# Convolving attention as 32-row strips: one 128-wide product per head replaced by 16 products of 32x32

## The reference

```python
attn = jnp.einsum('bhqd,bhkd->bhqk', q, k) * scale
...
kernels = jax.nn.softmax(kp.reshape(B, H, K1 * K2), axis=-1).reshape(B * H, 1, 3, 3)
attn0 = jnp.where(mask, 0.0, attn).reshape(1, B * H, T, T)
attn = lax.conv_general_dilated(attn0, kernels, window_strides=(1, 1), padding=((1, 1), (1, 1)),
                                feature_group_count=B * H, ...)
attn = jnp.where(mask, -jnp.inf, attn.reshape(B, H, T, T))
p = jax.nn.softmax(attn, axis=-1)
out = jnp.einsum('bhqk,bhkd->bhqd', p, v)
```

## Time and profile before

| what | value |
|---|---|
| median of 3 runs | 2318.37 us |
| the profiled execution, span of its instructions | 2345.7 us |
| TensorE busy, share of the span | 84% |
| stage "heads1", first to last instruction | 584.2 to 1138.6 us |

### The profile page before, as it was taken

The page is one execution under the profiler, slowest core; times in us unless marked ns, Lnnn a source line. Parts: engine busy times, 40 slices in busy tenths (PEclk is TensorE's granted clock), DMA queues, the critical chain, the costliest instruction groups (busy, mean ns, idle before and its releaser), DMA issues. The chain is left out here.

```text
span 2345.7 us, 41465 instructions
## 1 busy us (share of the span) xinstructions
PE 1968.9 (84%) x13179; PEld 1588.6 (68%) x13201; DVE 1255.6 (54%) x4235; ACT 921.3 (39%) x2196; POOL 776.1 (33%) x1055
## 2 busy tenths in 40 slices
PE   6859999987899999999849988994793797797594
PEld 5747766665798889989749975653582675454593
DVE  2542225633788888888420027975345445784423
ACT  3633321523233333333423345763342344575320
POOL 1012211110444444445211134410555646541132
PEclk9959999988899999999969999995896999899697
DMA  3213221000501110110069964426576475643294
GB/s 138 109 61 124 62 83 43 16 19 23 64 20 33 33 29 20 33 28 2 8 233 342 346 202 113 112 54 252 151 168 244 140 164 121 103 96 121 72 345 141
DMA packets 173404, 261.88 MB, mean 112 GB/s; under 512 B 23184, under 2 KB 138896, under 8 KB 169104
## 3 DMA queue, kind: packets, MB, share of 16 engines
q1 hardware_dynamic: 152272, 209.30, 28.0%
q0 software_dynamic: 16704, 45.64, 8.5%
q10 hardware_dynamic: 4224, 4.33, 0.9%
HBM read 181.19 MB, written 37.75 MB: 93 GB/s over the span
## 5 line engine op out<-in xcount | busy, mean ns | idle before, releaser
L2222 PE MATMUL heads_ps_c<-heads_band,heads_sT 128*128 128x129 f32 x3072 | 370.7, 277 | 13.3 <-DVE heads_band L2447 12.2
L2222 PEld LDWEIGHTS heads_ps_c<-heads_band,heads_sT 128*128 128x128 f32 x3072 | 356.9, 193 | 23.2 <-issue 21.3
L508 POOL DMA_INDIRECT weights_xg<-xn_rows,token_of x197 | 190.3, 966 | 444.8 <-DVE token_of L698 169.9
L2385 POOL TENSOR_SCALAR heads_band<-heads_shifts,heads_taps 128x130 f32<-128x130 f32 x384 | 253.1, 673 | 243.4 <-PE heads_ps_c L2222 239.8
L2315 ACT ACTIVATE heads_probs<-heads_mixes,heads_least 128x256 f32<-128x256 f32 x256 | 116.1, 500 | 344.9 <-DVE heads_least L2460 344.9
L2447 DVE SCALAR_TENSOR_TENSOR heads_band<-heads_shifts,heads_taps,heads_band 128x130 f32<-128x130 f32 x768 | 226.8, 351 | 19.0 <-POOL heads_band L2385 14.4
L1893 ACT ACTIVATE heads_probsT<-heads_ps_e 128x512 f32<-128x512 f32 x256 | 148.0, 597 | 70.0 <-PE heads_ps_e L1736 62.9
L1047 PE MATMUL experts_ps_g<-weights_w,experts_xT 128*128 x504 | 137.1, 396 | 9.1 <-ACT experts_xT L1097 6.9
L1070 PE MATMUL experts_ps_y<-weights_w,experts_hT 128*128 (+1 forms) x486 | 135.2, 387 | 4.3 <-ACT experts_hT L1111 1.7
L1712 PE MATMUL heads_ps_m<-heads_stackK,heads_stackQ 96*128 96x256 bf16 x512 | 101.3, 283 | 31.0 <-DMA heads_stackQ<-heads_q_pieces 12.4
L1104 ACT ACTIVATE experts_silu<-experts_ps_g 128x128 f32<-128x128 f32 (+1 forms) x165 | 53.3, 323 | 162.7 <-PE experts_ps_u L1052 77.8
(11 more groups left out here) (425 smaller groups left out, 4178.9 us busy)
## 6 DMA issues: line engine op xcount, KB each, us to landing
experts_w<-in_experts_dram SPq DMA_DIRECT2D x23, 2180.0 KB
weights_w<-in_experts_dram SPq DMA_DIRECT2D x32, 768.0 KB
weights_w<-in_experts_dram SPq DMA_DIRECT2D x14, 1536.0 KB
y_rows<-experts_y SPq DMA_DIRECT2D x125, 128.0 KB
heads_stackK<-heads_k_pieces SPq DMA_DIRECT2D x192, 64.0 KB, 2.7
heads_stackQ<-heads_q_pieces SPq DMA_DIRECT2D x192, 64.0 KB, 2.5
weights_w<-in_experts_dram SPq DMA_DIRECT2D x8, 1088.0 KB
xn_rows<-xn SPq DMA_DIRECT2D x4, 2048.0 KB, 7.5
```

The costliest lines, as they stand in the source:

```text
L508: pool.indirect_dma_start(self.xg[:, u, :], None, xn_dram, bass.IndirectOffsetOnAxis(ap=tb.token_of[:, j:j + 1], axis=0)).then_inc(self.x_ ...
L2222: last = pe.matmul(out[:, qc * SEQ + k0:qc * SEQ + k1], sT[:, h % 2, kc, qc * P + dq:qc * P + dq + P], band[:, h % 2, dq, w0:w0 + k1 - k0] ...
L2385: last = pool.tensor_scalar(band[:, h % 2, dq, :], shifts[:, 0, :], taps[:, r % 2, h, dq * TAPS:dq * TAPS + 1], None, ALU.mult)
```

## The change

The stage is written anew with strips. A sequence's 256 query rows are eight strips of 32 rows of which the inner 30 are kept, and a ninth that yields the last 16. A strip of one head lies on 32 partitions, four heads fill 128, and the band is a 32x32 matrix per tap column, so that a convolution is products of 32 rows by 32 columns: four heads on the array's four row groups, four strips on its four column groups. A step is four heads of a sequence (32 steps), or the ninth strips of all 16 heads of a sequence (8 steps). Scores come out with queries on partitions. ScalarE takes projections out of PSUM, GpSimd splits all rounds but the first two and builds the bands of a whole sequence at once. `ps_w` has four banks, `ps_s` two, `ps_o` (projections, values, mixes, turning back) and `ps_t` (transposes) one each. The context copies go; the loops are unrolled; the mask input grows from 1024 to 3072 bytes a partition; the inputs of the earlier shared-expert stage get a stage scope of their own.

```diff
-            def convolve(i, H):
...
-                        for dq in range(TAPS):
-                            last = pe.matmul(out[:, qc * SEQ + k0:qc * SEQ + k1],
-                                             sT[:, h % 2, kc, qc * P + dq:qc * P + dq + P],
-                                             band[:, h % 2, dq, w0:w0 + k1 - k0], ...)
+    STEPS = [(b, a) for b in range(B) for a in (None, 0, 1, 2, 3)]
+    pairs_of = lambda s: 2 if STEPS[s][1] is None else 4
...
+            def score(n, m):
...
+                if k >= 2:
+                    pe.wait_ge(masked, k - 1)
+                for half in range(2):
...
+                    for g in range(GH):
...
+                        last = pe.matmul(ps_s[LANE * g:LANE * (g + 1), k % 2, half * SEQ:(half + 1) * SEQ],
+                                         stackQ[:, u % SLOTS, first:first + LANE], stackK[:, u % SLOTS, j, :], ...)
+            def convolve(n):
+                pe.wait_ge(masked, pairs_before(n + 1))
...
+                for dk in range(TAPS):
+                    for g in range(GH):
+                        if dk == 0:
...
+                                pe.wait_ge(drained, 4 * (n - 1) + g + 1)
+                        rows = slice(LANE * g, LANE * (g + 1))
+                        for c in range(4):
...
+                                out = ps_w[LANE * c:LANE * (c + 1), g, :].rearrange("p (w n) -> p w n", w=2)
+                                band = bands[rows, b % 2, a, dk, :]
+                                src = sN[rows, group_of(n) % 2, c:c + 5:4, dk:dk + SEQ]
+                            last = pe.matmul(out, band, src, start=(dk == 0), stop=(dk == TAPS - 1), ...)
```

More of the change, by code:

```diff
@@ new lines, in conv_heads_stage @@
+        mask_add = s.sb("mask_add", [P, 3, SEQ])
+        near, taps = s.sb("near", [P, TAPS, LANE]), s.sb("taps", [P, B * GROUPS, TAPS * TAPS])
+        bands, product = s.sb("bands", [P, 2, GROUPS, TAPS, LANE]), s.sb("product", [P, 2, GROUPS, TAPS, LANE])
+        sN, sN9 = s.sb("sN", [P, 2, WINDOWS, SEQ + 2]), s.sb("sN9", [P, GROUPS, SEQ + 2])
+        mixes, probs, probsT = (s.sb(n, [P, GH, 2 * SEQ]) for n in ("mixes", "probs", "probsT"))
+        p9 = s.sb("p9", [P, GH, QC, GROUPS, NINTH])
@@ L2165, in _ @@
+            for u in range(ROUNDS):
+                stack(u, 0)
+                if u >= 2:
+                    stack(u, 1)
         @block.tensor
         def _(pe):
[L2167 to L2174, removed]
-                pe.wait_ge(v_placed, u + 1)
[L2176 to L2183, removed]
@@ L2240, in mix, with project @@
[L2240 to L2249 removed]
+            def project(u, n, out):
+                b, p = u // 2, u % 2
+                for c in range(DC):
+                    last = pe.matmul(out, (wq, wk)[n][:, c, p * P:(p + 1) * P], xnT[:, c, b * SEQ:(b + 1) * SEQ],
+                                     start=(c == 0), stop=(c == DC - 1))
+                last.then_inc(projected, 1)
@@ new lines, in _, with build_bands @@
+            steps.done(last)
+            def build_bands(b):
+                if b >= 2:
+                    pool.wait_ge(convolved, 4 * 5 * (b - 1))
+                shape = [P, GROUPS, TAPS, LANE]
+                tap = lambda dq: taps[:, GROUPS * b:GROUPS * (b + 1), dq * TAPS:(dq + 1) * TAPS].unsqueeze(3)\
+                    .to_broadcast(shape)
+                eye = lambda dq: near[:, dq, :].unsqueeze(1).unsqueeze(1).to_broadcast(shape)
+                band = bands[:, b % 2, :, :, :]
+                for dq, to in ((0, band), (1, product[:, 0, :, :, :]), (2, product[:, 1, :, :, :])):
+                    last = pool.tensor_tensor(to, tap(dq), eye(dq), ALU.mult)
+                steps.done(last)
+                for n in range(2):
+                    last = pool.tensor_tensor(band, band, product[:, n, :, :, :], ALU.add)
+                    if n == 0:
+                        steps.done(last)
+                last.then_inc(band_ready, 1)
@@ new lines, in drain @@
+            def drain(n, g):
+                v.wait_ge(convolved, 4 * n + g + 1)
+                if n > 0:
+                    v.wait_ge(exped, 4 * (n - 1) + g + 1)
+                for half in range(1 if STEPS[n][1] is None else 2):
+                    columns = slice(half * SEQ, (half + 1) * SEQ)
+                    last = v.tensor_tensor_reduce(out=mixes[:, g, columns], in0=ps_w[:, g, columns],
+                                                  in1=mask_add[:, 2 if STEPS[n][1] is None else half, :], scale=1.0,
+                                                  scalar=-NEG_BIG, op0=ALU.add, op1=ALU.min,
+                                                  accum_out=least[:, g, half:half + 1])
+                last.then_inc(drained, 1)
@@ L2490, in _ @@
-            for r in range(3):
-                for part in range(5):
-                    split(0, r, part)
-            loop(0, SLOTS)
-            first, per_loop = steps.n, ALL + SLOTS
-            with v.Fori(1, LOOPS - 1) as i:
-                steps.n = first + per_loop * (i - 1)
-                loop(i, SLOTS)
-            steps.n = first + per_loop * (LOOPS - 2)
-            loop(LOOPS - 1, 1)
-            row_max(LOOPS - 1, ALL - 1)
-            finish(LOOPS - 1, SLOTS - 1)
+                last.then_inc(finished, 1)
@@ new lines, in _ @@
+            v.wait_ge(edges_ready, 1)
+            for m in range(2):
+                drop_masked(0, m)
+            for n in range(len(STEPS) + 1):
+                before = STEPS[n - 1] if n else None
+                if n + 1 < len(STEPS):
+                    drop_masked(n + 1, 0)
+                    drop_masked(n + 1, 1)
+                if n < len(STEPS):
+                    drain(n, 0)
+                    drain(n, 1)
+                if n + 1 < len(STEPS) and pairs_of(n + 1) > 2:
+                    drop_masked(n + 1, 2)
+                    drop_masked(n + 1, 3)
+                if n < len(STEPS):
+                    drain(n, 2)
+                    drain(n, 3)
+                if before and before[1] in (1, 3):
+                    finish(group_of(n - 1) // 2)
```

690 lines of the change are left out of this document (366 added, 324 removed).

## The result

The changed kernel takes 2170.58 us (median of 4 runs, 2164.30 to 2171.71) against 2318.89 for the one before: a ratio of 0.9359, 95% interval 0.9344 to 0.9374. The forecast was 2145 with a range of 2095 to 2260. The saving is 148 us where 175 was forecast. The profiled execution before lay 27 us over the median of its runs, and that excess lies behind the changed stage (1207.1 us from the stage's end on, against 1180.4 in the trace after), so the stages of the two traces can be set against each other.

What follows compares the result with a forecast made beforehand. TensorE was taken to bound the stage: 23.5 start + 339 steps + 6 end = 368.5 for 554.4 us, 186 less; minus 10 for gaps and 1 for a boundary, 175 saved from 2318.4, said as 2145, range 2095 to 2260.

Steps and rivals of the forecast that it cites:

- What bounds the stage: In the convolving body of heads1 TensorE decides, 513.7 of 527.2 us; waits of VectorE, GpSimd or ScalarE cost nothing.
- The convolution: On TensorE, four heads' regular convolution takes 2.58 us, six rounds of 0.43 with all 16 products at once; a ninth 1.29.
- The chain of a step: TensorE and ScalarE hand over through single-bank tiles: a step 9.2 us with a = 2, 9.9 with a = 1 and 3.
- My 10 us for unexplained gaps: Taken off the stage's forecast saving of 186 us, for gaps that no wait explains.
- Rival 1: Row groups of a convolution don't overlap: 10.3 us each, 279 us more, 2424 us in all; chance 10%.
- Rival 2: Row groups overlap in part, eight products at once: convolution 5.16 us, 93 us more, 2238 in all; chance 15%.
- Rival 3: The clock falls because TensorE waits in every step: at 1.2 GHz half the time, 118 us more, 2263; chance 8%.

Runs made afterwards that it cites:

- two other orders of the places: Two edits of the changed kernel: column groups looped outside row groups, 2169.24 us; the second tap column's products in reverse order, 2167.15 us.
- copying twice: Changed kernel with ScalarE making each copy of turned probabilities in a regular step a second time, into a spare tile first: 2213.64 us.
- moving the scores: Changed kernel with the two scores that stand last in a step put ahead of the second head's transposes: 2153.76 us.

## Why the prediction was right, and its sizes

**What bounds the stage** was right. The time came out of TensorE's products. VectorE's 242 us and GpSimd's 159 us of work that went didn't count: 81 us put back on VectorE cost 2, while up to eight products at once in place of sixteen cost 110. No run put work back on GpSimd; for it there is only that no wait of TensorE in the view above ends with it.

**The convolution** was mis-sized. I took 6 rounds of 0.43 and a result 2.85 us after the start; it took 3.40, and a ninth one 2.13 for some 1.58. That is 0.55 in 40 steps, 22 of the 27 us by which the saving fell short. The working went from one row with four at once, and that row gave no hint: its 32 records are four products one after the other on each of four places, each with weights of its own, which load while the records before still run (timeline of the kernel before):

```profile
506.84 0.13 PEld L2682 LDWEIGHTS shared_ps_a<-shared_z,shared_w_cols 128*32 128x32 f32 x4 [0.30 <-issue]
...
507.27 0.13 PEld L2682 LDWEIGHTS shared_ps_a<-shared_z,shared_w_cols 128*32 128x32 f32 x4 [0.30 <-issue]
```

There the rounds stay 0.43 us apart through every new product, and so they do for a single row group of 32 rows (2.78 us a head). With sixteen at once each new tap column costs 0.19, and what comes once is 0.44, not 0.27. In the step above one load of the second tap column runs at 731.16 and the next only from 731.59 on, 0.88 us after the convolution's start. Why the others don't run earlier, as they do in the row of before, stays open: two other orders of the places made no difference.

96 records one after the other would be, by estimate from the rounds, 96 x 0.43 = 41.3 us and 0.16 by which the last outlasts its distance to the next (0.59 and 0.43). The measured 3.40 us is 12.2 times as fast. The Trainium skill, "TensorE: Matmul & The Clock Gate", Part 3, "Measured speedup vs the span model", has 10.6 for sixteen; by it the forecast was 2192 as against my 2145, and the measured 2171 lies between the two. The measurement decides: for these f32 products, in six rounds, it is 12.2.

**The chain of a step** was right in every link, as the timeline above shows, and copying twice and moving the scores agree with it from both sides. Behind the convolution it was 0.33 us too short in the step with a = 2: half of that lies in three changes of the array's shape (mix to transposes 1.00 us for 0.96, transposes to scores 0.59 for 0.54, scores to convolution 0.55 for 0.47), most of the rest in transposes whose result came after 0.66 us and not 0.60. A sequence is 47.15 us (the ninth convolutions start at 656.89 and 704.03) for 43.1, and the last two 44.87 for 40.1: 372.6 for 339. My 10 us for unexplained gaps cover a third of that, by luck: they were meant for something else and are as large as what the steps lack beside the convolutions (32 x 0.33). With the first convolution 25.3 us into the stage for 23.5 this makes the 25 us by which the stage is longer than forecast (404.1 for 379.5).

**Rival 1** (row groups in series) didn't come: the records stand 16 at a time. Issued in series the row groups still overlapped by two, for 2310; kept apart, they came with the lower clock, for 2808. Its price holds by the estimate from single heads: 11.4 us a convolution at the upper level for my 10.3, 289 us more than sixteen at once for my 279.

**Rival 2** (partial overlap) named 5.16 us for eight at once. Up to eight at once took 6.50; the changed kernel's 3.40 is far nearer to the 2.85 forecast for sixteen.

**Rival 3** (the clock falls) didn't come in the changed kernel: 1.0 from 615.0 to 983.6 us, with 44 us of gaps. The runs with fewer row groups at once did have the lower clock, with hardly a gap on TensorE; copying twice had it too, in short stretches (0.96 over 615 to 1020 us), with more waits than the changed kernel. So the gaps that I looked at don't tell the cases apart by themselves.

## What to carry to other kernels

When a stage's product gets three times shorter, the order of what follows sets the next bound: follow one step link by link, with the buffers that have only one bank, and put work that waits for nothing into each wait (17 us here from moving two calls). A row with four products at once doesn't price sixteen: beside the rounds there came 0.19 us for each new tap column, whatever the columns, and 0.44 once, where four at once had no such pause and 0.20. Rivals may come together: fewer row groups at once cost overlap here, and came with the lower clock; a stretch of each level in the same trace tells the two apart.

## What the runs showed of the hardware beyond that

Issued row group by row group, f32 products on 32 by 32 places still ran two row groups at once without any help (6.50 us where 10.3 were expected). New weights cost nothing with four places at once (rounds 0.43 us apart) and 0.19 us with sixteen. With one row group at work the granted clock was 0.63 while TensorE was busy 191 of 200 us, and with two it was 0.50 through whole convolutions, busy 12.00 of 12.00 us, and 1.00 in others. With four it was 0.99 over the body, TensorE busy 329.5 of 374 us, and 0.96 with the copies doubled. Why it differs wasn't tried.
